# Five edits to a one-core network kernel: bias rows on 16 partitions, category loads written out, tokens as the stationary operand, token bias and rows tile moved, last softmax inside the value tree

## The reference, cut to what matters

```
# layer 0, first part
h = relu(x @ W1[lang] + b1[lang]) @ W2[lang] + b2[lang]     # per language of the sequence
c = norm(x + h) * gamma[lang] + beta[lang]
x = x + attention(c)                # 16 heads of 8, rope over heads, softmax over 32 keys, @ Wo.T + bo
# layer 0, second part
c2 = einsum('bli,bio->blo', x, weight[category]) + bias[category]   # 64 categories, one per sequence
x = x + mole(relu(mole(c2, W1, ...)), W2, ...)                      # 128 -> 512 -> 128 with routed LoRA
# layer 1, first part
y = experts(x)                      # 4 + 3 feed-forward nets 128 -> 512 -> 128, gated
x = x + eight_blocks(y)             # linear attention and feed-forward, biases bq bk bv bo b1 b2, two norms each
# layer 1, second part
y = experts2(x)                     # 3 + 2 feed-forward nets, gated
q, k, v = tree_q(y), tree_k(y), tree_v(y)     # 16 leaves of width 64 each, one leaf chosen per token
x = x + softmax(q @ k.T / sqrt(128)) @ v      # within each sequence
```

## Time and profile before

| What | us |
|---|---|
| timed runs, median of three | 685.86 (681.86, 685.86, 686.48) |
| profiled execution | 680.64 |
| its span | 678.8 |
| TensorE matmuls busy | 600.4 (88%) |
| VectorE busy | 427.5 (63%) |
| ScalarE busy | 318.6 (47%) |
| POOL busy | 117.5 (17%) |

### The profile page before, as it was taken

The page is one execution under the profiler, slowest core; times in us unless marked ns, Lnnn a source line. Parts: engine busy times, 40 slices in busy tenths (PEclk is TensorE's granted clock), DMA queues, the critical chain, the costliest instruction groups (busy, mean ns, idle before and its releaser), DMA issues.

```text
span 678.8 us, 9349 instructions
## 1 busy us (share of the span) xinstructions
PE 600.4 (88%) x3234; PEld 417.3 (61%) x3234; DVE 427.5 (63%) x1024; ACT 318.6 (47%) x504; POOL 117.5 (17%) x94
## 2 busy tenths in 40 slices
PE   9576898999989898889898989888869989999996
PEld 4356767877775455546463746455558778455595
DVE  5999433476776667575848485766644776653444
ACT  4064122443435566575656565756633433444341
POOL 0320023042400111104111321111110452200000
PEclk9799979999999899999999999999988998999997
DMA  3011295500005001010101010010000000000000
GB/s 94 23 43 44 52 294 140 112 0 1 0 1 154 1 0 48 1 47 2 47 0 47 0 47 0 16 30 0 1 1 1 1 0 1 0 1 0 1 1 31
DMA packets 43867, 21.83 MB, mean 32 GB/s; under 512 B 14642, under 2 KB 40941, under 8 KB 43834
## 3 DMA queue, kind: packets, MB, share of 16 engines
q1 hardware_dynamic: 43834, 21.40, 11.8%
HBM read 20.79 MB, written 0.52 MB: 31 GB/s over the span
## 4 chain that ended last, share of the span: by engine, by line
PE 62%; DVE 26%; ACT 5%; issue 4%; POOL 2%; DVEq 0%; ACTq 0%; POOLq 0%
PE ps L1596 8%; PE ps L1529 7%; PE ps L1512 7%; PE ps L1602 5%; PE ps L1716 5%; PE ps L1734 4%; PE ps L1557 3%; PE ps L1574 2%; PE ps L1266 2%; PE ps L1582 2%; DVE stat L834 2%; PE ps L1740 2%; DVE z L1029 2%; POOL rstd L497 2%; DVE yt L828 2%
## 5 line engine op out<-in xcount | busy, mean ns | idle before, releaser
L497 POOL TENSOR_TENSOR rstd<-rv,minus_half 128x4 f32<-128x4 f32 x34 | 47.6, 1401 | 288.6 <-DVE rv L843 288.6
L1070 DVE SCALAR_TENSOR_TENSOR zr<-ps,zr 128x512 fp32r<-128x512 f32 x96 | 63.9, 688 | 50.0 <-ACT zr L670 49.7
L670 ACT ACTIVATE zr<-ps 128x512 fp32r<-128x512 f32 x96 | 57.4, 598 | 80.2 <-PE ps L1512 76.3
L1602 PEld LDWEIGHTS ps<-wl,z 128*128 128x128 f32 x512 | 64.0, 192 | 17.5 <-ACT z L732 8.7
L1596 PE MATMUL ps<-cf,wl 128*128 128x512 f32 x128 | 66.6, 623 | 7.0 <-ACT cf L578 7.0
L1602 PE MATMUL ps<-wl,z 128*128 128x128 f32 x512 | 68.4, 277 | 0.0
L828 DVE TENSOR_TENSOR yt<-ps,z 128x512 f32<-128x512 f32 x32 | 22.1, 692 | 72.9 <-ACT z L737 43.7
L1529 PE MATMUL ps<-zr 128*128 128x512 f32 x192 | 61.4, 402 | 6.3 <-DVE zr L1070 6.3
L1512 PE MATMUL ps<-zr 128*128 128x512 f32 x192 | 62.0, 405 | 1.4 <-DVE zr L1011 1.4
L1223 DVE SCALAR_TENSOR_TENSOR z<-z,kc 128x512 f32<-128x512 f32 x48 | 34.5, 751 | 44.5 <-ACT z L785 43.1
L785 ACT ACTIVATE z<-ps,cols 128x512 f32<-128x512 f32 x48 | 32.9, 688 | 48.6 <-PE ps L1716 48.3
(11 more groups left out here) (251 smaller groups left out, 1086.6 us busy)
## 6 DMA issues: line engine op xcount, KB each, us to landing
wl<-in_L_attn_W SPq DMA_DIRECT2D x16, 256.0 KB
big<-in_L_cond_weight SPq DMA_DIRECT2D x32, 64.0 KB, 1.8
arena<-in_L_cond_expert_wi SPq DMA_DIRECT2D x1, 1024.0 KB, 6.2
arena<-in_L_cond_expert_wo SPq DMA_DIRECT2D x4, 256.0 KB, 7.1
big<-in_L_ffn_q_w SPq DMA_DIRECT2D x2, 512.0 KB, 5.2
big<-in_L_ffn_k_w SPq DMA_DIRECT2D x2, 512.0 KB, 7.1
tree_v<-in_L_ffn_v_w SPq DMA_DIRECT2D x2, 512.0 KB, 7.0
arena<-in_L_cond_share_wi SPq DMA_DIRECT2D x1, 768.0 KB, 6.9
```

The costliest lines, as they stand in the source:

```text
L497: nc.gpsimd.tensor_tensor(rstd[:, half, :], rv[:, half, :], minus_half[:, :], ALU.pow).then_inc(S_["rstd"], 1)
L670: nc.scalar.activation(hidden_part(h, n, 0), ps[h][:, n % 2, :], ACT.Relu).then_inc(S_[k + "_hi"], 1)
L1070: V.scalar_tensor_tensor(hidden_part(h, n, 1), ps[h][:, n % 2, :], 0.0, hidden_part(h, n, 0), ALU.max, ALU.subtract).then_inc(S_[k + "_lo" ...
L1602: ins = T.matmul(ps[h][:, 2, tok(h, i)], z(h, c)[:, tok(h, i)], wl[s][:, 4 * D + FF + c * D:4 * D + FF + (c + 1) * D], start=False, stop=( ...
```

## The change

1. `row_bias` and its three parts lie on 16 partitions with 128 numbers each instead of on one with 2048; casts and subtractions stay five.
2. SyncE's order is now: `row_bias`, category loads written out as 32 pieces of straight code, the three moves into `bias3` behind the eighth of them, mixture weights, experts' weights, gate weights, then the 14 loads of `rows`, then layers 0 and 1.
3. POOL adds the token bias ahead of the norm's roots, from `xt[0]` into `xt[1]`, after the language masks; the attention's residual adds to `xt[1]`.
4. TensorE turns `rows` behind the second LoRA output of half 0 instead of ahead of the first norm's turns, into another bank; ScalarE copies it to `cols` there; the `keep_warm(6)` there uses another bank.
5. The category product loads the 32 tokens of a sequence and streams its 128 x 128 matrix, each sequence into one of four 32-column strips. The result has tokens on partitions, so ScalarE copies it to `xn` and TensorE turns it back.
6. The scores are made behind round `SCORED` = 19; their softmax is spread over VectorE's and ScalarE's rounds 19 to 22.

```diff
+SCORED = (TREES - 1) * LFC + 3
...
-        row_bias = Z[1][0:1, 4:8, :].rearrange("p a n -> p (a n)")
-        row_parts = Z[1][0:1, 8:14, :].bitcast(BF16).rearrange("p a n -> p (a n)")
+        row_bias = Z[1][0:2 * LAYERS, 4, 0:D]
+        row_parts = Z[1][0:2 * LAYERS, 8, :].bitcast(BF16)
...
-            sp.wait_ge(S_["p_rb"], 5)
-            for part in range(3):
-                load(bias3[part:part + 1, :, :].rearrange("p l d -> p (l d)"), row_part(part), "ld_rb")
-
-            sp.wait_ge(S_["ld_ids"], 48)
-            with sp.Fori(0, B) as b:
-                cat = sp.value_load(ids[0:1, 1, bass.ds(b, 1)], min_val=0, max_val=CATS - 1)
-                sp.dma_start(w_cat[:, bass.ds(b, 1), :],
...
+            for b in range(B):
+                cat = sp.value_load(ids[0:1, 1, b:b + 1], min_val=0, max_val=CATS - 1)
+                sp.dma_start(w_cat[:, b:b + 1, :],
+                             I["L0_cond2_weight"][bass.ds(cat, 1), :, :].rearrange("a p n -> p a n")
+                             ).then_inc(S_["ld_cat"], 16)
+                if b == 7:
+                    sp.wait_ge(S_["p_rb"], 5)
+                    for part in range(3):
+                        load(bias3[part:part + 1, :, :], row_part(part), "ld_rb")
...
+            pool.wait_ge(S_["ld_b"], 16 * 5)
+            pool.wait_ge(S_["a_mask"], 2 * LCH)
+            for h in HALVES:
+                nc.gpsimd.tensor_tensor(xt[1][:, h], xt[0][:, h], token_bias[:, :].unsqueeze(1).to_broadcast([P, TILES, D]),
+                                        ALU.add).then_inc(S_["p_pool"], 1)
             for h in HALVES:
                 root(h + 1, h)
-            pool.wait_ge(S_["ld_b"], 16 * 5)
...
-            pe.wait_ge(S_["ld_rows"], 16 * (LV + TREES))
-            turn(ps[1][:, 1, :], [rows[:, :]], "p_mm")
-
-            pe.wait_ge(S_["p_mmc"], PREP["cols"])
...
             pe.wait_ge(S_["ld_cat"], 16 * B)
             for h in HALVES:
-                pe.wait_ge(S_["b_xf"], h + 1)
+                pe.wait_ge(S_["c_act"], h + 1)
                 for b in range(HB):
-                    ins = T.matmul(batch(ps[h][:, 0, :], b), w_cat[:, h * HB + b, :], batch(xf[:, h], b),
-                                   start=True, stop=True)
-                ins.then_inc(S_["c_mm"], 1)
+                    i, q = divmod(b, P // S)
+                    ins = T.matmul(ps[h][q * QUAD:(q + 1) * QUAD, 0, tok(h, i)], batch(xf[:, h], b), w_cat[:, h * HB + b, :],
+                                   start=True, stop=True, tile_position=(0, q * QUAD))
+                ins.then_inc(S_["c_pe"], 1)
+            for h in HALVES:
+                pe.wait_ge(S_["c_act"], 2 + h + 1)
+                turn(ps[h][:, 2, :], [xn[:, h, i, :] for i in range(TILES)], "c_pe")
...
             lora_out(0)
+            pe.wait_ge(S_["ld_rows"], 16 * (LV + TREES))
+            turn(ps[1][:, 2, :], [rows[:, :]], "p_mm")
...
-            keep_warm(6, ps[1][:, 2, :])
+            keep_warm(6, ps[0][:, 3, :])
...
                 if n >= 1:
                     leaf_output(n - 1)
...
+                if n == SCORED:
+                    for h in HALVES:
+                        final_scores(h)
```

On VectorE the rounds of the trees get three additions; on ScalarE the exponential moves into round `SCORED + 1`:

```diff
+                if n == SCORED - 2:
+                    for h in HALVES:
+                        own.step(V.memset(z(h, 12), 0.0))
+                if n == SCORED:
+                    for h in HALVES:
+                        final_scores(h)
+                if n in (SCORED + 2, SCORED + 3):
+                    final_probabilities(n - SCORED - 2)
```

More of the change, by code:

```diff
@@ L358, in row, with load_mixture, load_ffns @@
                 return I[name].rearrange("(a n) -> a n", a=1)
+            def load_mixture():
+                load(gvec[:, 0, :], I["L1_cond_gate_vecs"], "ld_gv")
+                for e in range(ME):
+                    load(ar1[:, e * MR:(e + 1) * MR], I["L0_ffn_A1"][e], "ld_d")
+                    load(w2f[:, :, D + e * MR:D + (e + 1) * MR], I["L0_ffn_A2"][e].rearrange("(c p) r -> p c r", p=P), "ld_d")
+                load(ar1[:, MER:MER + ME], I["L0_ffn_R1"], "ld_d")
+                load(w2f[:, :, D + MER:D + MER + ME], I["L0_ffn_R2"].rearrange("(c p) e -> p c e", p=P), "ld_d")
+                sp.wait_ge(S_["k_mem"], 6)
+                for r in range(0, 3 * QUAD, QUAD):
+                    load(lora[r:r + MER, 0:FF], I["L0_ffn_B1"].rearrange("e r n -> (e r) n"), "ld_d")
+                    load(lora[r + MER:r + MER + 1, 0:FF], row("L0_ffn_b1"), "ld_d")
+                    load(lora[r:r + MER, FF:], I["L0_ffn_B2"].rearrange("e r n -> (e r) n"), "ld_d")
+                    load(lora[r + MER:r + MER + 1, FF:], row("L0_ffn_b2"), "ld_d")
+                load(w1f[:, :], I["L0_ffn_W1"], "ld_d")
+                load(w2f[:, :, 0:D], I["L0_ffn_W2"].rearrange("(c p) n -> p c n", p=P), "ld_d")
+            def load_ffns(wi, wo, n, at, sem):
+                load(arena[:, at:at + n, 0, :], I[wi][0:n].rearrange("e d f -> d e f"), sem)
+                for e in range(n):
+                    load(arena[:, at + e, 1, :].rearrange("p (c n) -> p c n", c=FC),
+                         I[wo][e].rearrange("(c p) n -> p c n", p=P), sem)
             load(kc[:, 0:K_GOAL], konst[:, 0:K_GOAL], "ld_const")
@@ L414, in _ @@
-            for r in range(0, 3 * QUAD, QUAD):
-                load(lora[r:r + MER, 0:FF], I["L0_ffn_B1"].rearrange("e r n -> (e r) n"), "ld_d")
-                load(lora[r + MER:r + MER + 1, 0:FF], row("L0_ffn_b1"), "ld_d")
-                load(lora[r:r + MER, FF:], I["L0_ffn_B2"].rearrange("e r n -> (e r) n"), "ld_d")
-                load(lora[r + MER:r + MER + 1, FF:], row("L0_ffn_b2"), "ld_d")
-            load(w1f[:, :], I["L0_ffn_W1"], "ld_d")
-            load(w2f[:, :, 0:D], I["L0_ffn_W2"].rearrange("(c p) n -> p c n", p=P), "ld_d")
@@ L654, in _ @@
                 mixture_out(1, h)
+            act.wait_ge(S_["p_mm"], PREP["cols"])
+            copy(cols[:, :], ps[1][:, 2, 0:P], "p_mmc")
             act.wait_ge(S_["p_mm"], PREP["coef"])
@@ L1233, in _, with final_probabilities @@
                                 ).then_inc(S_["h_sub"], 1)
[L1234 removed]
+            def final_probabilities(h):
                 dve.wait_ge(S_["h_exp"], h + 1)
@@ L1747, in leaf_output, with final_scores @@
                         ins.then_inc(S_["h_acc"], 1)
+            def final_scores(h):
+                pe.wait_ge(S_["h_accc"], 2 + h + 1)
+                for b in range(HB):
+                    i, q = divmod(b, P // S)
+                    r = slice(q * QUAD, (q + 1) * QUAD)
+                    ins = T.matmul(ps[h][r, 3, i * S:(i + 1) * S], batch(z(h, 0), b), batch(z(h, 1), b),
+                                   start=True, stop=True, tile_position=(0, q * QUAD))
+                ins.then_inc(S_["h_s"], 1)
             for n in range(TREES * LFC + 1):
@@ L1755, in _ @@
                     leaf_output(n - 1)
-            for h in HALVES:
-                pe.wait_ge(S_["h_accc"], 2 + h + 1)
-                for b in range(HB):
-                    i, q = divmod(b, P // S)
-                    r = slice(q * QUAD, (q + 1) * QUAD)
-                    ins = T.matmul(ps[h][r, 0, i * S:(i + 1) * S], batch(z(h, 0), b), batch(z(h, 1), b),
-                                   start=True, stop=True, tile_position=(0, q * QUAD))
-                ins.then_inc(S_["h_s"], 1)
+                if n == SCORED:
+                    for h in HALVES:
+                        final_scores(h)
             for h in HALVES:
```

80 lines of the change are left out of this document (31 added, 49 removed).

## The result

The changed kernel takes 663.46 us (median of 661.63, 663.40, 663.52 and 665.57) against 685.75 beside it: a ratio of 0.9708, 95% interval 0.9665 to 0.9751 (the two medians alone divide to 0.9675). The forecast was 666, with a range from 656 to 674. Its profiled execution took 663.40 us, 661.6 between first and last instruction, at a mean granted clock of 0.982; before, had a span of 678.8 at 0.961.

A forecast was written before the change was run, and what follows sets the result against it. Bounds: VectorE in the front, TensorE at the category product, a lone VectorE softmax at the end. Terms 5.5 + 8.0 - 0.2 + 5.2 = 18.5 us, off the median 685.86 give 667.4, off the mean 683.71 665.2; forecast 666, range 656 to 674.

The forecast's parts named there:

- Front: bias rows: Front, VectorE: five bias instructions on 16 partitions let the first residual start at 18.50 instead of 23.13; gain 4.6 us.
- Front: clock: Front, TensorE: shorter pause may keep query and key products at 2.4 GHz; gain 0.9 us, ends 0 and 1.8.
- Loads, hidden: SyncE's loads: at 1.3 us per category load, all reordered loads land before they are wanted; no gain or loss counted.
- Category product: Product through hidden product: 64 passes in 2.8 us, LoRA and hidden product mostly at full clock; gain 8.0 us.
- a serial case: Category product: passes follow one another at 0.117 us each, 7.5 us for 64; gain 2.4 to 3.8 us.
- Rows turn: Middle: turning the rows tile moves onto TensorE's path behind the second LoRA output, 2 passes; loss 0.2 us.
- End: End: softmax moved into rounds, last residual of half 1 at 670.2 instead of 675.39; gain 5.2 us, 3 at low clock.
- Sum: Whole kernel: front 5.5, category product 8.0, middle -0.2 and end 5.2 make a gain of 18.5 us.
- (a): Category product: strips don't overlap and the clock stays low; gain 12.0 us, about 672 us; chance 0.11.
- (b): End: VectorE's added work makes masks late in rounds 21 to 23, TensorE waits; gain 13.3, about 671 us; chance 0.10.
- (c): SyncE: written-out loads above 1.56 us each make the mixture's last load late; slower, about 692 us at 2.4; chance 0.03.
- (d): Whole kernel: full clock everywhere and strips in parallel, gain 23 us, about 661 us; chance 0.12.

The follow-up runs named there:

- same strip: Changed kernel with four category products in a row into the same 32-column strip, then the next strip: 664.55 us, ratio 0.9731.
- softmax behind: Changed kernel with final scores and softmax behind the tree network's last round again, as before: 670.49 us, ratio 0.9816.
- one-partition bias: Changed kernel with the bias rows on one partition of 2048 again: 668.44 us, ratio 0.9796.
- loops: Changed kernel with its 32 category loads in two loops (8 and 24 passes), places in SyncE's order kept: 662.91 us, ratio 0.9693.
- the last three: Changed kernel with third tree's 16-row products at the head of its sums, 665.44 us; 15 more filler passes, 663.33; GpSimd's first expert splits held back, 665.63.
- the first of the tries: Changed kernel with the third tree's 16-row products issued at the head of that tree's sums, not their end: 665.44 us, ratio 0.9715.

## Why the prediction was right

**Front: bias rows, 4.6 us.** Confirmed. The residual waits for TensorE; from the language network's matmul to the residual it was 7.44 us before and is 2.92 now, a gain of 4.5. Two of the five small instructions took 1.2 us beside POOL; the five took 3.2 us instead of 1.1, within the factor of four allowed, and were done by 18.98, ahead of TensorE's half at 19.56.

**Front: clock, 0.9 of 1.8 us.** Under-sized. Both products ran at full clock and gave 3.66 - 1.98 = 1.68. So the front gave 6.1 (counted to the first queries) for a forecast of 5.5.

**Loads, hidden.** Right, with 1.10 us per load where I had 1.3; with the loop's price the load was still hidden, narrowly as I wrote, by 1.95 us. I had drawn the hiding correctly but not its worth: the prediction books the new order at nothing, and with SyncE's block as before 11.3 us of the gain are gone. Had I asked what the old order does to a category product that begins 5 us earlier and is 7 us shorter, the old rows would have answered: its last mixture load released POOL at 86.50.

**Category product, 8.0 us.** The point I counted to, start to hidden product, came out at 5.36 where I had 5.6. I misread where the old time came from: the prediction puts the half clock into the LoRA and hidden products and names the row from 84 to 86 us for it, but the 64 passes ran until 87.06, so that row lies inside them. Of the 7.3 us gained up to the hidden product, 2.1 are clock in the old product and 1.5 are clock in the LoRA passes (3.41 to 1.94); the form gave 3.7. That the short product also escaped the low clock was in the sum only because both end points were read from rows, which is luck as much as reasoning. The pass price was mis-sized in the other direction than feared: 1.99 us for 64 passes where I took 2.8, and a serial case of 4.3 where I had 7.5. The hidden product gave nothing: 6.93 us against 5.2 at full clock and 6.58 before. That is the term that failed in this profile, and it hangs on the execution: with tokens stationary and no wait ahead of it, seven of the runs (same strip, softmax behind, one-partition bias, loops, and the last three) show it at full clock.

The Trainium skill, TensorEngine Tiling (Array Packing), Performance Considerations, pairs this swap with a column tiling of four where 32 columns are streamed, and speaks of a TensorE speedup of four behind it. The runs agree with that as an upper bound: about 7.1 / 1.99 = 3.6 at full clock, of which 7.1 / 4.3 = 1.7 needs no alternating strips. (The plain quotient, 9.18 / 1.99 = 4.6, divides a product partly at half clock by one at full clock.) The drain at a change of mode that the same page has in section Key Properties shows in no row as a cost that can be told apart: the product begins 0.14 us behind ScalarE's copy in both forms.

**Rows turn, 0.2 us.** The turn stands on the chain with 0.13 us. Right.

**End, 5.2 us.** The mechanism held: TensorE waited for no mask in rounds 21 to 23, the scores cost 0.69 us for a forecast of 0.9. The gain was 4.41 - 0.69 = 3.7, since the last passes ran at half clock: 3.58 us instead of 1.9. I had given 3 us for that case as the lower end. With the softmax alone the same passes took 2.00.

**Sum.** 18.5 us forecast, 17.2 in the profiles: 0.6 more in the front, 0.1 more in the attention, 1.0 less in category and hidden product (7.31 - 0.35 for 8.0), 1.5 less at the end, 1.0 less before the change's first instruction, 0.1 more up to the gate passes; 1.5 more between there and the leaves' end once the scores are counted apart. That last figure is 2.0 us lost at the experts' start and 3.5 won further on, in stretches where no instruction changed and the clock was higher (0.97 against 0.92 from 470 to 580 us). So the mechanism of each part held, but the closeness of the sum is in part luck: misses of 1 to 2 us, most of them clock, cancelled. By median, 22.3, the forecast was 2.5 us too high; how much of these 2.5 is the median of before, drawn from four executions, the runs can't say.

**Rivals.** (a) fell with the 1.99 us. (b) fell with the masks. (c) fell with 1.10 us per load; but its place, the mixture's last load ahead of the LoRA product, was the right one to watch: that is where both kernels with the old order and the quick product wait. (d) had the product right and the clock wrong in the profile; by its time, 661, it was as near to the median of 663.46 as the forecast was.

## What to carry to other kernels

When a stage gets shorter, read when its inputs land under the old order of issues, and move the loads with the stage: here the same product brought the hidden product 7 us nearer or 1, depending on when one load landed. Where a loop of loads is hidden, writing it out gives nothing. A bound on a TensorE pass has to be taken from a row with the same width of stationary operand, not only of streamed columns: 0.111 us with 128 loaded and 32 streamed, 0.117 with 128 and 128, 0.067 with 32 and 128. And before two times are divided, read the granted clock of both: a stage that spans a fall of the clock has two prices in it.

## What the runs showed that was not expected

- A pass with 32 stationary and 128 streamed columns costs 0.067 us on one strip and 0.031 on alternating strips; with 128 stationary and 32 streamed it costs about 0.111 at full clock (45 passes in 5.0 us) and 9.18 / 64 = 0.143 as a mean over a fall of the clock.
- A short VectorE copy slowed from 0.26 to 2.19 us while POOL worked on two-operand additions, and POOL's own pair of additions went from 2.62 to 5.36 us when VectorE ran long casts beside it.
- Kernels that differ by nothing near the second experts differ there by several us of half-clock time. The changed kernel spreads over 3.9 us from run to run and the three tries over 5.8 to 6.4: with the first of the tries, runs at a mean clock of 0.969 took 667.1 to 667.4 us, the others, at 0.981 to 0.987, 661.0 to 663.8. What starts such a stretch in one execution and not in the next stays open.
